# Stages between four attention layers rebuilt, and second-layer units moved to other slots

## The reference

```python
x = x + jnp.tanh(g_xattn[i]) * attention_i(_layernorm(x), ctx)
x = x + jnp.tanh(g_ffn[i]) * ffn_i(_layernorm(x))
```

## Time and profile before

| | |
|---|---|
| median of 3 runs | 2248.95 us (2247.39 to 2251.37) |
| profiled execution | 2255.36 us, its span 2253.6 us |
| busy: PE | 1992.7 us, 88% |
| busy: DVE | 1463.5 us, 65% |
| busy: ACT, POOL | 1020.2 us (45%), 900.4 us (40%) |
| PE in 40 slices | `4999999999638899998887999996789999999996` |
| its clock | `9999999999868999999888999999798999999998` |

### The profile page before, as it was taken

How to read it: one execution, slowest core, us unless ns; L and a number is a source line. 1 busy time by engine, 2 the same in 40 slices (tenths; PEclk the granted TensorE clock), 3 DMA queues, 4 the chain that set the end, 5 groups by cost and what they waited for, 6 DMA issues and landing times.

```text
span 2253.6 us, 33253 instructions
## 1 busy us (share of the span) xinstructions
PE 1992.7 (88%) x10874; PEld 1666.5 (74%) x10874; DVE 1463.5 (65%) x2737; ACT 1020.2 (45%) x2256; POOL 900.4 (40%) x955
## 2 busy tenths in 40 slices
PE   4999999999638899998887999996789999999996
PEld 3788888887436777777565888886578888888874
DVE  4777777777567777776433556554467776677774
ACT  1666666666314444443112544442145555455550
POOL 1545555554225555454321323321234444344430
PEclk9999999999868999999888999998799999999998
DMA  3122222121120211110211101001201110111101
GB/s 134 33 82 72 85 70 70 54 73 52 57 70 29 76 47 51 47 47 20 88 36 36 29 11 32 22 1 34 70 10 43 43 44 15 48 43 43 34 1 43
DMA packets 47021, 106.77 MB, mean 47 GB/s; under 512 B 6016, under 2 KB 21888, under 8 KB 43056
## 3 DMA queue, kind: packets, MB, share of 16 engines
q1 hardware_dynamic: 46896, 105.14, 14.9%
HBM read 98.37 MB, written 6.75 MB: 47 GB/s over the span
## 4 chain that ended last, share of the span: by engine, by line
PE 63%; DVE 18%; ACT 8%; issue 7%; DMA 3%; POOL 1%; SPq 1%; ACTq 0%; DVEq 0%; POOLq 0%
PE psX L366 21%; PE psQ L366 12%; PE psS L366 11%; PE psO L366 10%; PE psT L689 5%; DVE pT_lo L841 1%; PE psT L366 1%; DVE dq_space L454 1%; ACT pT_hi L1019 1%; DVE nmax L829 1%; DVE p_sb L823 1%; ACT oT_hi L1041 1%; DVE nbias L827 1%; ACT dq_space L441 1%; DVE nbias L817 1%
## 5 line engine op out<-in xcount | busy, mean ns | idle before, releaser
L1124 POOL TENSOR_SCALAR p_sb<-p_sb,rrec 128x512 f32<-128x512 f32 (+1 forms) x320 | 265.8, 831 | 703.6 <-DVE rrec L837 703.5
L1019 ACT ACTIVATE pT_hi<-psT 128x512 fp32r<-128x512 f32 (+2 forms) x384 | 235.1, 612 | 385.1 <-PE psT L689 385.0
L841 DVE TENSOR_TENSOR pT_lo<-psT,pT_hi 128x512 fp32r<-128x512 f32 (+2 forms) x384 | 271.2, 706 | 82.2 <-ACT pT_hi L1019 82.2
L366 PE MATMUL psO<-pT_hi,v_hi 128*128 128x256 f32 (+1 forms) x832 | 257.0, 309 | 69.9 <-DVE oT_lo L862 33.9
L689 PE MATMUL psT<-ident,p_sb 128*128 128x128 f32 x1600 | 244.3, 278 | 12.4 <-POOL p_sb L1124 9.2
L366 PE MATMUL psO<-pT_lo,v_hi 128*128 128x256 f32 (+1 forms) x832 | 238.6, 287 | 0.0
L366 PE MATMUL psO<-pT_hi,v_lo 128*128 128x256 f32 (+1 forms) x832 | 238.5, 287 | 0.0
L689 PEld LDWEIGHTS psT<-ident,p_sb 128*128 128x128 f32 x1600 | 196.8, 143 | 51.5 <-POOL p_sb L1124 14.0
L366 PEld LDWEIGHTS psO<-pT_hi,v_hi 128*128 128x128 f32 (+1 forms) x832 | 156.4, 188 | 85.2 <-issue 40.3
L366 PE MATMUL psQ<-xnT_hi,wq_hi 128*128 128x512 f32 (+1 forms) x448 | 191.5, 427 | 17.2 <-POOL wq_lo L1131 16.4
L1012 ACT ACTIVATE p_sb<-psS,nbias 128x512 f32<-128x512 f32 (+1 forms) x192 | 145.3, 757 | 126.1 <-DVE nbias L831 126.1
(11 more groups left out here) (325 smaller groups left out, 4753.7 us busy)
## 6 DMA issues: line engine op xcount, KB each, us to landing
wq_f<-in_a_wq SPq DMA_DIRECT2D x96, 256.0 KB, 2.7
wo_f<-in_a_wo SPq DMA_DIRECT2D x24, 1024.0 KB, 5.4
wkv_f<-in_a_wkv SPq DMA_DIRECT2D x24, 512.0 KB, 3.8
mask_sb<-in_codes SPq DMA_DIRECT2D x32, 174.0 KB, 2.5
qscr<-in_amax SPq DMA_DIRECT2D x32, 174.0 KB, 2.3
w<-qscr SPq DMA_DIRECT2D x32, 174.0 KB, 1.9
wo_f<-in_f_wT SPq DMA_DIRECT2D x3, 1024.0 KB, 5.1
wq_f<-in_a_wq SPq DMA_DIRECT2D x16, 192.0 KB, 2.3
```

Source lines behind the costliest of these rows:

```text
L366: mm = pe.matmul(dst, w, m, start=(first and k == 0), stop=(last and k == n - 1))
L841: L.t_lo.inc(dve.tensor_tensor(pT_view(L, pT_lo, j), t_view(L, j), pT_view(L, pT_hi, j).bitcast(F32), ALU.subtract))
L1019: L.t_hi.inc(act.activation(pT_view(L, pT_hi, j), t_view(L, j), ACT.Copy))
L1124: L.s_norm.inc(pool.tensor_scalar(p_view(L, j), p_view(L, j), rrec[:, j:j + 1], 1.0, ALU.mult, ALU.mult))
```

## The change

- **Start**: `x` is loaded first; the context goes to four buffers and is split by ACT and DVE (first part POOL), after and beside the LN; `ones` is loaded last.
- **Early loads**: each layer's first loads wait for the counters of the buffers that they overwrite in place of `x_ready`; `first_high` and `first_low` split the first weights there.
- **F0**: loads and both threshold passes (now into `kT_lo`, `kT_hi`) go into the attention layer, around its last `o_low`. Bias, scale, statistics and normalise go tile by tile; gamma and beta go to POOL.
- **F1**: weights are loaded and split inside the attention layer; `up` is cut in `up_main` and `up_lora`; the low-rank product stands behind `up_main(0)`.
- **F2**: A and the router get tiles of their own and are split before; the base product stands ahead of the transposes of the top-2 chain.
- **F3**: loads, low-rank product, mixing and splits (ACT and POOL) go into the attention layer, ahead of its last output projections.
- **End**: each tile is stored as it is ready (`out_ready`), 256 KB each.
- **Second layer**: output units 1 and 2 in (1,0), 3 in (1,1); `v0` from (2,1) to (3,0), `t0` from (3,0) to (3,1).

```diff
-OUT_PAIRS = {(0, 1): [0], (1, 0): [1], (1, 1): [2, 3]}
+OUT_PAIRS = {(0, 1): [0], (1, 0): [1, 2], (1, 1): [3]}
-         prep={(2, 0): ["k0"], (2, 1): ["v0"], (3, 0): ["t0"]}),
+         prep={(2, 0): ["k0"], (3, 0): ["v0"], (3, 1): ["t0"]}),
...
+        ctx_f = [p_sb[:, 0:1024], p_sb[:, 1024:2048], flat(scr[:, :, :]), flat(qscr[:, :, :])]
+
         def start_sync(sp):
+            sp.dma_start(x_sb[:, :, :], a["x"].rearrange("b (t p) d -> p (b t) d", p=P)).then_inc(x_dma, 16)
             sp.dma_start(ident[:, :], a["c_ident"]).then_inc(const_dma, 16)
-            sp.dma_start(ones[:, :], a["c_ones"]).then_inc(const_dma, 16)
-            sp.dma_start(x_sb[:, :, :], a["x"].rearrange("b (t p) d -> p (b t) d", p=P)).then_inc(const_dma, 16)
             sp.dma_start(gates[:, 0:4], a["g_xattn"].partition_broadcast(P)).then_inc(gate_dma, 16)
             sp.dma_start(gates[:, 4:8], a["g_ffn"].partition_broadcast(P)).then_inc(gate_dma, 16)
+
+        def start_sync_ctx(sp):
             for c in range(DC):
-                if c >= 2:
-                    sp.wait_ge(ctx_lo, c - 1)
-                sp.dma_start(p_sb[:, (c % 2) * 1024:(c % 2 + 1) * 1024],
-                             a["ctxT"][:, c, :]).then_inc(ctx_dma[c % 2], 16)
+                sp.dma_start(ctx_f[c], a["ctxT"][:, c, :]).then_inc(ctx_dma[c], 16)
+            sp.dma_start(ones[:, :], a["c_ones"]).then_inc(const_dma, 16)
 
         def start_vector(dve):
-            dve.memset(half[:, :], -0.5).then_inc(half_done, 1)
-            for c in range(DC):
-                dve.wait_ge(ctx_dma[c % 2], 16 * (c // 2 + 1))
-                f = p_sb[:, (c % 2) * 1024:(c % 2 + 1) * 1024]
-                dve.tensor_copy(cT_hi[:, c, :], f).then_inc(ctx_hi, 1)
+            for c in range(1, DC):
                 dve.wait_ge(ctx_hi, c + 1)
-                dve.tensor_tensor(cT_lo[:, c, :], f, cT_hi[:, c, :].bitcast(F32), ALU.subtract).then_inc(ctx_lo, 1)
-            dve.wait_ge(ctx_lo, DC)
+                dve.tensor_tensor(cT_lo[:, c, :], ctx_f[c], cT_hi[:, c, :].bitcast(F32),
+                                  ALU.subtract).then_inc(ctx_lo, 1)
 
         def start_scalar(act):
...
+        def start_ctx_high(act, c):
+            act.wait_ge(ctx_dma[c], 16)
+            act.activation(cT_hi[:, c, :], ctx_f[c], ACT.Copy).then_inc(ctx_hi, 1)
+
+        def start_gpsimd(pool):
+            pool.wait_ge(ctx_hi, 1)
+            pool.tensor_tensor(cT_lo[:, 0, :], ctx_f[0], cT_hi[:, 0, :].bitcast(F32), ALU.subtract).then_inc(ctx_lo0, 1)
...
+                if k == 8:
+                    dve.sem_inc(out_ready, 1)
...
+        FIRST_W = (("wq", 0), ("wq", 1), ("wkv", 0), ("wkv", 1))
+
+        def first_high(act, L):
+            if L.i == 2:
+                act.wait_ge(f1_up, H1C)
+            for kind, piece in FIRST_W:
+                if L.i == 2 and kind == "wkv":
+                    act.wait_ge(f1_down, H1C)
+                w_high(act, L, kind, Group(0), piece)
+
+        def first_low(pool, L):
+            for kind, piece in FIRST_W:
+                w_low(pool, L, kind, Group(0), piece)
...
+            def first():
+                if L.i == 1:
+                    layers[0].wq_lo.wait(sp, 4 * layers[0].n)
+                    layers[0].wkv_lo.wait(sp, 2 * layers[0].n)
+                elif L.i == 2:
+                    sp.wait_ge(f1_lo, H1C)
+                    sp.wait_ge(f1_dlo, H1C)
+                elif L.i == 3:
+                    layers[2].wq_lo.wait(sp, 4 * layers[2].n)
+                    layers[2].wkv_lo.wait(sp, 2 * layers[2].n)
+                load_wq(Group(0), 0)
+                load_wkv(Group(0))
+                if L.i == 0:
+                    start_sync_ctx(sp)
+                load_wq(Group(0), 1)
+
+            first()
+            if L.i == 0:
+                sp.dma_start(rows[:, :], a["L0_xattn_bo"].partition_broadcast(P)).then_inc(row_dma, 16)
+            if L.i == 1:
+                sp.wait_ge(dq_done, 32)
+            if L.i == 3:
+                sp.wait_ge(x_ready, 7)
             if "vecs" in names:
                 L.vec_dma.inc(sp.dma_start(vecs[:, 0:names["vecs"].shape[1]], names["vecs"]), 16)
             if L.masked:
                 L.vec_dma.inc(sp.dma_start(mask_sb[:, 0:names["mask"].shape[1]], names["mask"]), 16)
+            load_wq(Group(0), 2)
...
+                if L.i == 0:
+                    f0_threshold(dve)
+                elif L.i == 1:
+                    f1_up_high(dve, 0)
+                    f1_up_high(dve, 1)
+                    f1_down_high(dve, 0)
+                elif L.i == 2:
+                    f2_router(dve)
                 o_low(g, 3)
+                if L.i == 0:
+                    f0_ternary(dve)
+                elif L.i == 3:
+                    f3_mixed(dve)
...
+            def tail(g):
+                if L.i == 1:
+                    f1_up_low(pool, 0)
+                    f1_up_low(pool, 1)
+                    f1_down_low(pool, 0)
+                elif L.i == 3:
+                    f3_low(pool)
...
+        f0_hi, f0_ge_sb = ([z[:, c // 2, (c % 2) * D:(c % 2 + 1) * D] for c in range(DC)] for z in (kT_hi, kT_lo))
+
+        def f0_sync(sp, L):
+            L.wo_lo.wait(sp, 4 * L.n)
+            sp.dma_start(wo_f[:, :, :], a["f0_wT"]).then_inc(f0_wdma, 16)
+            L.q_lo.wait(sp, 4 * L.n)
+            sp.dma_start(vecs[:, 0:1], a["L0_ffn_quant_scale"].partition_broadcast(P)).then_inc(f0_dma, 16)
+            L.t_mm.wait(sp, L.group_slots * L.n)
             for i, z in enumerate(("bias", "scale", "ln_gamma", "ln_beta")):
                 sp.dma_start(p_sb[:, i * D:(i + 1) * D], a[f"L0_ffn_{z}"].partition_broadcast(P)).then_inc(f0_dma, 16)
...
+        def f0_threshold(dve):
+            dve.wait_ge(f0_wdma, 16)
+            dve.tensor_scalar(flat(kT_lo[:, :, :]), flat(wo_f[:, :, :]), 0.1, None, ALU.is_ge).then_inc(f0_ge, 1)
+
+        def f0_ternary(dve):
+            dve.wait_ge(f0_ge, 1)
+            dve.scalar_tensor_tensor(flat(kT_hi[:, :, :]), flat(wo_f[:, :, :]), -0.1,
+                                     flat(kT_lo[:, :, :]).bitcast(F32), ALU.is_le, ALU.subtract,
+                                     reverse1=True).then_inc(f0_w, 1)
...
+            def normalise(t):
+                dve.wait_ge(f0_pow, t + 1)
+                dve.tensor_scalar(y[t], y[t], ln_mv[:, t, 0:1], ln_rstd[:, t:t + 1],
+                                  ALU.subtract, ALU.mult).then_inc(f0_xn, 1)
+
             for t in range(NT):
                 dve.wait_ge(f0_mm, t + 1)
-                ins = dve.tensor_tensor(y[t], f0_banks[t], bias, ALU.add)
-            after(dve, ins)
+                after(dve, dve.tensor_tensor(y[t], f0_banks[t], bias, ALU.add))
+                after(dve, dve.tensor_tensor(y[t], y[t], scale, ALU.mult))
+                after(dve, dve.bn_stats(ln_stat[:, t, :], y[t]))
+                after(dve, dve.bn_aggr(ln_mv[:, t, :], ln_stat[:, t, :]))
+                dve.tensor_scalar(ln_var[:, t:t + 1], ln_mv[:, t, 1:2], EPS, None, ALU.add).then_inc(f0_var, 1)
+                if t:
+                    normalise(t - 1)
+            normalise(NT - 1)
...
+            pow_(0)
             for t in range(NT):
-                ins = dve.tensor_tensor(y[t], y[t], scale, ALU.mult)
...
-            for t in range(NT):
-                ins = dve.tensor_tensor(y[t], y[t], gamma, ALU.mult)
-            after(dve, ins)
-            for t in range(NT):
-                dve.tensor_tensor(y[t], y[t], beta, ALU.add).then_inc(f0_y, 1)
...
-
-        def f0_gpsimd(pool):
-            pool.wait_ge(f0_var, 1)
-            pool.tensor_tensor(ln_rstd[:, :], ln_var[:, :], half[:, :], ALU.pow).then_inc(f0_pow, 1)
+                if t + 1 < NT:
+                    pow_(t + 1)
+                pool.wait_ge(f0_xn, t + 1)
+                pool.tensor_tensor(y[t], y[t], gamma, ALU.mult).then_inc(f0_gamma, 1)
+                pool.wait_ge(f0_gamma, t + 1)
+                pool.tensor_tensor(y[t], y[t], beta, ALU.add).then_inc(f0_y, 1)
...
+        def f1_sync(sp, L):
+            L.wq_lo.wait(sp, 4 * L.n)
+            L.wkv_lo.wait(sp, 2 * L.n)
...
+            up_main(0)
+            pe.wait_ge(f1_lsplit, 1)
+            three(pe, psQ[0:RANK, :], [([z[:, m * RANK:(m + 1) * RANK] for z in la], (xnT_hi[:, m, :], xnT_lo[:, m, :]))
+                                       for m in range(DC)]).then_inc(f1_lmm, 1)
+            up_main(1)
+            up_lora(0)
+            up_lora(1)
             for c, n in enumerate(f1_rows):
-                if c + 1 < H1C:
-                    up(c + 1)
+                if 2 <= c + 1 < H1C:
+                    up_main(c + 1)
+                    up_lora(c + 1)
...
+        f2_out_banks = [psX[:, 0, :], psX[:, 1, :], psQ[:, :], psO[:, :]]
+        f2_tp_bank = psT[:, 0, :]
+        ar_f, ar_hi, ar_lo = (z[:, 0:DC * AR] for z in (mask_sb, flat(kx_hi[:, :, :]), flat(kx_lo[:, :, :])))
+        f2_b_f, f2_b_hi, f2_b_lo = qscr[:, 0, :], kT_hi[:, 0, 0:D], kT_lo[:, 0, 0:D]
...
```

(121 more changed lines are left out.)

255 lines of the change are left out of this document (94 added, 161 removed).

## The result

The changed kernel takes 2223.9 us (median of 4 runs, 2221.2 to 2230.7), the kernel before 2249.0: a ratio of 0.9892, 95% interval 0.9866 to 0.9918. Forecast were 2190 us and a range of 2172 to 2208: faster, as said, but by 25 us instead of 59. Its profiled execution, 2221.2 us with a span of 2219.4, is the fastest of the four; against the profiled one of before it gained 34.2 us of span.

A forecast was written before the change was run, and what follows sets the result against it. PE was taken as the bound, by turns with DVE in the second layer, and idle at start, joints and end. Gains of 69.0 us less 9.5 lost gave 59.5, so 2190 us; range 2172 to 2208 (8 in 10).

The forecast's parts named there:

- Start: Before the first attention layer: loading `x` first lets LN and the first projection begin earlier; gain 12 us.
- F0: First joint between layers: waits for loads and threshold passes go, gamma and beta move to POOL; gain 18 us (14 to 21).
- F1: Second joint: `up_main(0)` starts when LN is done; gain 5.3 us (4 to 7.6), plus 2.9 for `wq_lo` behind it.
- F2: Third joint: base product runs under the top-2 chain; gain 15.2 us (12.5 to 20), 2.9 of it for `wq_lo`.
- F3: End of the kernel: low-rank products ahead of the last output projections, smaller last store; gain 15.6 us (13 to 17.8).
- the second layer's slots: Second attention layer: moving `v0` and `t0` lengthens the `oT_lo` wait by 1.35 us in seven groups; loss 9.5, bounds 0 and 12.
- I charge the lower level at each resume, as before: At the joints, PE was taken to resume at 1.2 GHz each time, as in the kernel before.
- The outputs' part of the step: Second layer: moving output units costs 0, since PE does the same work in another order and DVE keeps up.
- The stages: Start, joints and end together, without the second layer's slots: 69.0 us gained.
- rival (c): POOL and DVE hold each other up in F0, with bad ends of Start and F1: 2201 us, chance 0.2.
- the 2.9 of `wq_lo`: Behind F1, the next layer's projection no longer waits for `wq_lo`, only for LN's 1.4 us: gain 2.9 us.
- Rival (b): The second layer's slot move costs nothing, or the clock stays up through the joints: 2180 us, chance 0.27.

The follow-up runs named there:

- e4: The changed kernel, with PE repeating v0's twelve products, unneeded, in its wait for `kT_lo` in (2,1) of the second layer: 2211.8 us, ratio 0.9815.
- e9: The kernel of e1, with only the transposes `t0` moved from (3,0) to (3,1) in the second layer: 2212.9 us, ratio 0.9822.
- e3: The changed kernel with only the second layer's outputs back in their old slots, `v0` and `t0` left in the new ones: 2224.0 us, ratio 0.9876.
- e1: The changed kernel with the second layer's outputs, `v0` and `t0` back in their old slots, all rebuilt stages kept: 2196.0 us, ratio 0.9749.
- e8: The kernel of e1, at the start with LN's four powers ahead of `wq_lo` on POOL and all four context low parts on DVE: 2198.7 us, ratio 0.9761.
- e6: The kernel of e1, with F0's multiplication by gamma and addition of beta on DVE instead of POOL: 2197.1 us, ratio 0.9754.
- e7: The kernel of e1, with three of four heads of the second layer's output unit 0 done in PE's wait for `oT_lo`: 2186.1 us, ratio 0.9691.

## Why the prediction was wrong

**The step that failed is the second layer's slots**, "whose wait grows by 1.35 from 3.23, in each of seven groups: loss 9.5", with the bound of 12 above it. The idle time in it was nearly right: 1.7 us a group in the profile after. What is missing is the clock. The forecast treated it in a part of its own, and there only for the joints: "I charge the lower level at each resume, as before". Inside the layer it was taken to stay up, though the trace of the kernel before has waits of the same 3.2 us with a dip behind them and without one: the period from 833.34 took 49.4 us, that from 882.75 took 47.9. By the six periods above, the step cost 1.6 us of idle time and 2.3 of clock each, where 1.35 and nothing were forecast. Run e4 shows the clock's part by itself, with DVE's order left as it is. The Trainium skill (TensorE: Matmul & The Clock Gate, Why this matters for your kernels) warns of just this: idle gaps of PE between bursts of matmuls drop the clock in the middle of a kernel. The forecast did not weigh it inside the layer; this case's rows agree with it, 0.69 and 0.58 behind waits of 3.40 and 3.54 us, and they also hold waits of 3.2 us behind which the clock stayed up.

**How the move makes two waits.** The forecast said that the copy taken out of (2,1) "shortens nothing, since the next scores wait for `kT_lo` anyway". True for DVE, and the point for PE was missed: `v0`'s 2.7 us of products were what PE did *during* that wait. Without them it grew from 0.8 to 3.5 us. PE's idle time in sum grew by less than that, since the products now fill the wait in (3,0), which was 1.3; but a wait behind which the clock had stayed up became one behind which it falls. So the forecast also had its idle time at the wrong wait: that for `oT_lo`, where it put all of it, grew by 0.2 only. The other move, `t0`, is what lengthened the wait for `oT_lo`, from 3.23 to 3.40 us, and the dips behind it became nearly regular (e9). Of the 28 us, e9 has 17 with `t0` alone; that `v0` makes the other 11 is the difference, not a run of its own. The outputs' part of the step, 0, held (e3).

**The stages** gave 57 us by the medians of e1, and 61 by the table, against 69, each near its term:

- Start, 9.7 against 12, just below its bound of 10. LN ended at 20.4 instead of 15.6, for DVE waited 2.9 us for a power that POOL had queued behind `wq_lo`, and one of its passes took 2.48 us beside POOL's subtraction. But e8 removed both, and its first `o_low` came no earlier, so what held the end of this stretch back stays open.
- F0, 14.0 against 18. PE resumed at once and at the upper clock (1.00 in 594 to 601 us), better than forecast. But rival (c) held in its mechanism: DVE passes beside POOL's were stretched, and e6 shows that the move of gamma and beta gave nothing. By the rule of the Trainium skill (GPSIMD Engine Reference, Key points) that the two share their SBUF interfaces this was to be expected, and this case's passes agree: 1.50 us in the mean beside POOL, 0.69 alone.
- F1, 5.8 against 8.2. The first down product began 14.8 us after LN's last transposes (1082.2 to 1097.0), where the forecast allowed 15.3 and the kernel before took 21.6: 6.8 gained. But the stretch ahead took 17.8 us instead of 16.1, since eight output products ran at the lower clock, 0.43 us each instead of 0.23. With the 2.9 of `wq_lo` that makes 8.0, so some 2.2 were lost behind the first down product, which had waited 1.8 us for `q_lo`; where, was not tried.
- F2, 16.3, and F3 with the end, 15.1, lie on their terms. The base product ran under the top-2 chain, and F3's 48 products took 11.2 us wholly at the upper clock. The last stores cost 2.5 us behind the last update, where 2.9 was taken.

So the 34 us between 2190 and 2224 part like this. The slots are 19: with the measured 28.8 in place of 9.5 the forecast's own sum is 2209, at the upper edge of the range. The stages' shortfall (63 with the third layer's 2.4, against 69) makes it 2215. The remaining 9 are the level, and no mechanism: the forecast took off 6.4 us for the profiled execution of before, which lay over its median, while that of after lies 2.7 under its own. Rival (b), the slots free or the clock up through the joints, was half right at the joints (F0 and F3) and wrong in the layer. None of the rivals had the clock falling inside a layer.

## What to carry to other kernels

Before a unit is moved out of a slot, ask what wait it covered, not only what it delays: a wait that grows from short to long may also cost the clock behind it. Read idle time and busy time of PE for the same number of matmuls; if busy time grows, the granted clock is the place to look. And work that stands right behind a long wait is worth splitting, so that the part which needs nothing of what is waited for fills it (e7).

## What the runs showed of the hardware

The cost of a wait of PE was not smooth. Where it was 3.23 us, the clock fell behind it in some groups (periods of 49.5 us) and not in others (47.9); where it was 3.40, in nearly all; where it was 3.54 in the changed kernel, in all. It is not a limit at one length either: one wait of 3.38 us in e8 (resume at 761.10) was followed by a period of 47.9 us at a mean clock of 1.00, and one of 3.40 in e4 (970.12) by one of 49.1. A dip cost about 1.6 us in the kernel before, and more in e9. Filling the wait with 84 matmuls that nobody needs made the kernel 12 us faster.

Passes of DVE that take 0.42 to 0.75 us on 512 columns alone took 1.2 to 1.8 us beside POOL passes with two operands in SBUF, so that moving eight of them to POOL was worth nothing. Not all of them did: the statistics (L1328) and the bias pass, which reads PSUM (L1326), stayed at 0.69 us in the same stretch.
